# Nine small pieces of the blocks' weights, one an iteration, behind the evacuation of heads

## The reference, cut to what matters

```
x = x + gate_a * (attend(ln_mod(x) @ W_qkv + b_qkv) @ W_proj + b_proj)
x = x + attend(ln(x) @ W_qc + b_qc, context @ W_kvc + b_kvc) @ W_cproj + b_cproj
x = x + gate_m * (gelu(ln_mod(x) @ W_mlp1 + b_mlp1) @ W_mlp2 + b_mlp2)
```

## Time and profile before

| | |
|---|---|
| median of three runs | 2992.5 us (2986.59 to 2997.8) |
| the profiled execution | 2997.99 us |
| its span | 2996.2 us |
| TensorE busy | 2816.4 us (94%) |
| VectorE, ScalarE, GpSimd busy | 59%, 51%, 23% |
| mean granted TensorE clock | 0.96 |

### The profile page before, as it was taken

The page is one execution under the profiler, slowest core; times in us unless marked ns, Lnnn a source line. Parts: engine busy times, 40 slices in busy tenths (PEclk is TensorE's granted clock), DMA queues, the critical chain, the costliest instruction groups (busy, mean ns, idle before and its releaser), DMA issues. The chain is left out here.

```text
span 2996.2 us, 61868 instructions
## 1 busy us (share of the span) xinstructions
PE 2816.4 (94%) x23508; PEld 2298.0 (77%) x23508; DVE 1761.6 (59%) x3583; ACT 1535.1 (51%) x2701; POOL 700.9 (23%) x760
## 2 busy tenths in 40 slices
PE   5999999994899999999999999999999999999997
PEld 4999999993577777777777776777777777777766
DVE  1344444433567756766766756676675676666642
ACT  2444444432365546556556555556555655655653
POOL 3334443321121212212212211122121221221211
PEclk8999999996799989999999998999999999999998
DMA  5122111003343344444453443434445444444421
GB/s 166 64 76 88 67 67 39 24 8 112 71 109 103 94 108 98 103 102 119 111 130 93 109 101 99 101 88 112 120 98 135 99 94 110 96 94 109 98 63 34
DMA packets 276262, 277.90 MB, mean 93 GB/s; under 512 B 90176, under 2 KB 205232, under 8 KB 275968
## 3 DMA queue, kind: packets, MB, share of 16 engines
q1 hardware_dynamic: 260176, 251.24, 33.7%
q10 hardware_dynamic: 15792, 22.70, 2.5%
HBM read 99.03 MB, written 29.56 MB: 43 GB/s over the span
## 5 line engine op out<-in xcount | busy, mean ns | idle before, releaser
L1538 ACT ACTIVATE p_f<-score 128x1024 f32<-128x1024 f32 (+1 forms) x576 | 560.7, 1019 | 369.4 <-PE obank L2159 175.7
L1815 DVE TENSOR_REDUCE m_a<-score 128x4 f32<-128x1024 f32 x384 | 457.6, 1217 | 58.8 <-PE score L2125 58.7
L2229 PE MATMUL gbank<-w,h_c 128*128 128x256 f32 x1536 | 414.2, 405 | 1.2 <-ACT h_c L1555 0.9
L2229 PEld LDWEIGHTS gbank<-w,h_c 128*128 128x128 f32 x1536 | 283.7, 197 | 51.1 <-issue 1.3
L959 PE MATMUL m_ps<-m_comb,m_w 128*128 128x256 f32 x2304 | 300.5, 286 | 0.0
L959 PEld LDWEIGHTS m_ps<-m_comb,m_w 128*128 128x128 f32 x2304 | 284.8, 190 | 3.1 <-issue 1.7
L1419 POOL TENSOR_TENSOR res_a<-res_a,bias_a 128x512 f32<-128x512 f32 x48 | 64.7, 1347 | 710.0 <-DMA bias_a<-rows_L 710.0
L632 ACT ACTIVATE m_hf<-m_ps,tab 128x256 f32<-128x256 f32 x192 | 80.5, 470 | 252.7 <-PE m_ps L959 252.7
L2159 PE MATMUL obank<-p_f,v_s 128*20 128x256 f32 x3072 | 206.9, 401 | 0.0
L574 POOL TENSOR_TENSOR m_hhl<-m_hf,m_hhl 128x512 fp32r<-128x512 f32 x96 | 125.3, 1305 | 327.8 <-DVE m_hhl L798 327.8
L1825 DVE TENSOR_REDUCE m_b<-gbank 128x4 f32<-128x308 f32 x192 | 92.2, 480 | 170.8 <-PE gbank L2174 108.9
(11 more groups left out here) (234 smaller groups left out, 5627.9 us busy)
## 6 DMA issues: line engine op xcount, KB each, us to landing
k_cat<-k_hl SPq DMA_DIRECT2D x288, 128.0 KB, 3.6
q_cat<-q_hl SPq DMA_DIRECT2D x288, 128.0 KB, 4.0
qc_cat<-qc_hl SPq DMA_DIRECT2D x288, 128.0 KB, 3.2
split_L<-m_cut SPq DMA_DIRECT2D x24, 512.0 KB, 5.3
x_a<-x_after_L SPq DMA_DIRECT2D x48, 256.0 KB, 4.0
res_a<-x_after_L SPq DMA_DIRECT2D x48, 256.0 KB, 2.8
kc_cat<-kc_hl SPq DMA_DIRECT2D x288, 39.0 KB, 1.9
x_after_L<-y_c SPq DMA_DIRECT2D x32, 256.0 KB, 3.2
```

Of the source, the lines that this page charges most:

```text
L1538: e.activation(p_f[i % 4][0:n, :], score[i % 2].ap[0:n, :, :].rearrange("p h n -> p (h n)"), ACT.Exp, scale=SCALE).then_inc(ex.sem, 1)
L1815: e.tensor_reduce(m_a[:, :, i::NPAIR].rearrange("p t h -> p h t"), score[i % 2].ap[:, :, :].rearrange("p h (t k) -> p h t k", t=TT), AX.X, ...
L2229: mm = e.matmul(B_DOWN.ap[:, tt, :], h_c[:, k, tt * P:(tt + 1) * P], weights_of(d)["w2"][:, k, :], start=(k == 0), stop=(k == MC - 1))
```

## The change

The two-place weights come in nine loads a layer: the three spread biases, `w_kvc` in two halves (256 KB each) and `w2` in four pieces (256 KB each). `next_rest` issues one of them an iteration, in n = 6 to 14 for layer 2 and n = 23 to 31 for layer 3, and its place in ScalarE's list is behind `self_heads(a, 0)`. `next_up_high` stands behind it. `next_self_out` moves behind `self_heads(a, 1)`, `next_queries_keys` behind `cross_max_high`, and `next_up_low` to the end of the previous iteration, behind `cross_keys_high`. The bias columns of all three layers get buffers of their own and are loaded by SyncE in layer 0, in its iterations 8 to 17. SyncE's loads for layer 1 come in the same nine pieces, in iterations 2 to 6.

```diff
-            loads.append((w["bv"][:, :], spread(bv)))
-            loads.append((w["bvc"][:, :], spread(bvc)))
-            loads.append((w["boc"][:, :], spread(p["boc"])))
-            side_by_side(w["kvc"], p["kvc"])
-            loads.append((w["w2"][:, :, :], chunks(p["w2"])))
+            loads = [(w[k][:, :], spread(b)) for k, b in (("bv", bv), ("bvc", bvc), ("boc", p["boc"]))]
+            for i in range(2):
+                loads.append((w["kvc"][:, :, i * D:(i + 1) * D], chunks(kvc[i])))
+            for i in range(0, MC, 2):
+                loads.append((w["w2"][:, i:i + 2, :], chunks(p["w2"][i * P:(i + 2) * P, :])))
             return loads
+
+        def column_loads(L):
+
+            p = layer_parts(L)
+            if L < 3:
+                b = [p["bqkv"][0:D], p["bqkv"][D:2 * D], p["bqc"], p["bkvc"][0:D]]
+            else:
+                b = [p["bq"], p["bk"], p["bqc"], p["bkc"]]
+            return ([(bcols[L][:, 2 * i:2 * i + 2], column(b[i])) for i in range(4)]
+                    + [(bcols[L][:, 8:16], column(p["b1"]))])
...
-        n_w = [0, 10, 10, 11]
+        n_w = [0, 9, 9, 9]
...
+                if n >= 8:
+                    for dst, src in columns[n - 8::N_ITER - 8]:
+                        e.dma_start(dst, src).then_inc(S["col"].sem, 16)
...
-                                      bias=weights_of(u)["bcol"][:, at + m:at + m + 1])
+                                      bias=bcols[layer(u)][:, at + m:at + m + 1])
...
-                if 6 <= n < 11:
-                    for dst, src in layer_loads(2)[n - 6::5]:
+                if 6 <= n < 15:
+                    for dst, src in layer_loads(2)[n - 6::9]:
                         e.dma_start(dst, src).then_inc(s_w[2], 16)
...
-                if NB + 7 <= n < NB + 13:
-                    for dst, src in layer_loads(3)[n - NB - 7::6]:
+                if NB + 7 <= n < NB + 16:
+                    for dst, src in layer_loads(3)[n - NB - 7::9]:
                         e.dma_start(dst, src).then_inc(s_w[3], 16)
...
                 exp_table(n - 6)
-                next_self_out(n - 4)
-                next_rest(n)
-                next_up_low(n - 6)
                 self_weights(a, 0)
                 self_weights(a, 1)
                 queries_high(n - 2)
                 self_weights(a, 2)
                 self_weights(a, 3)
-                next_up_high(n - 6)
                 self_weights(a, 4)
                 self_weights(a, 5)
                 self_weights(a, 6)
                 self_weights(a, 7)
+                cross_max_high(b)
                 next_queries_keys(n - 2)
-                cross_max_high(b)
+                self_heads(a, 0)
                 next_cross_queries(n - 4)
-                self_heads(a, 0)
+                next_rest(n)
+                next_up_high(n - 6)
                 self_heads(a, 1)
+                next_self_out(n - 4)
                 next_cross_out(n - 5)
...
                 cross_keys_high(a)
+                next_up_low(c)
                 self_modulated(q)
```

More of the change, by code:

```diff
@@ L107, in build @@
         cond_siluT = sbr("cond_siluT", [P, CC, NB])
+        bcols = [None] + [sbr(f"b_col{i}", [P, 16]) for i in (1, 2, 3)]
         tabs = [None] + [sbr(f"tab{i}", [P, NB, 8]) for i in (1, 2, 3)]
@@ L112, in layer_buffers @@
             return dict(
-                kvc=sb(f"w_kvc{i}", [P, CC, 2 * D]), w2=sb(f"w_2{i}", [P, MC, D]), bcol=sb(f"b_col{i}", [P, 16]),
+                kvc=sb(f"w_kvc{i}", [P, CC, 2 * D]), w2=sb(f"w_2{i}", [P, MC, D]),
                 bv=sb(f"b_v{i}", [P, D]), bvc=sb(f"b_vc{i}", [P, D]), boc=sb(f"b_oc{i}", [P, D]))
@@ L142, in layer_loads @@
         def layer_loads(L):
[L144 to L150, removed]
+            w, p = WT[L % 2], layer_parts(L)
             if L < 3:
-                bq, bk, bv = (p["bqkv"][i * D:(i + 1) * D] for i in range(3))
-                bkc, bvc = (p["bkvc"][i * D:(i + 1) * D] for i in range(2))
-            else:
[L156 to L159, removed]
-            loads.append((w["bv"][:, :], spread(bv)))
-            loads.append((w["bvc"][:, :], spread(bvc)))
-            loads.append((w["boc"][:, :], spread(p["boc"])))
-            side_by_side(w["kvc"], p["kvc"])
-            loads.append((w["w2"][:, :, :], chunks(p["w2"])))
-            return loads
+                bv, bvc = p["bqkv"][2 * D:3 * D], p["bkvc"][D:2 * D]
+                kvc = [p["kvc"][0][:, at:at + D] for at in (0, D)]
+            else:
+                bv, bvc, kvc = p["bv"], p["bvc"], p["kvc"]
+            loads = [(w[k][:, :], spread(b)) for k, b in (("bv", bv), ("bvc", bvc), ("boc", p["boc"]))]
[3 more added lines that the diff above has]
+                loads.append((w["w2"][:, i:i + 2, :], chunks(p["w2"][i * P:(i + 2) * P, :])))
+            return loads
+        def column_loads(L):
[6 more added lines that the diff above has]
+                    + [(bcols[L][:, 8:16], column(p["b1"]))])
         def own_load(L, k):
@@ L183, in build @@
             mixture(nc, t, mix, layer_loads(1), s_w[1],
-                    [own_load(1, k) for k in ("o", "oc")], pieces(1) + pieces(2) + pieces(3), split, xs[0], rows, consts, chunks, spread, by_tile, buffers)
+                    [own_load(1, k) for k in ("o", "oc")], pieces(1) + pieces(2) + pieces(3), split,
+                    column_loads(1) + column_loads(2) + column_loads(3), xs[0], rows, consts, chunks, spread, by_tile, buffers)
         WT[0] = layer_buffers(root, 0)
-        blocks(nc, t, xs, tabs, rows, ident, half, eps5, eps6, WT, s_w, n_w, layer_loads,
+        blocks(nc, t, xs, tabs, bcols, rows, ident, half, eps5, eps6, WT, s_w, n_w, layer_loads,
                W, W_in, split, own_load, by_tile, buffers)
@@ L406, in _, with mixture @@
             e.tensor_scalar(mix["b2"][:, 2, :], ps_b[1][:, 0, :], 0.5, None, ALU.mult).then_inc(s_done, 1)
-def mixture(nc, t, mix, loads_L1, s_w1, own_L1, raw_pieces, split, x_out, rows, consts, chunks, spread, by_tile, buffers):
+def mixture(nc, t, mix, loads_L1, s_w1, own_L1, raw_pieces, split, columns, x_out, rows, consts, chunks, spread, by_tile, buffers):
     from concourse import mybir
@@ L460, in mixture @@
                         ve=1, rstd=1, nxlo=1, evlo=1, hl=6, y=1, cuthi=1, cutlo=1),
-                    dma=dict(x0=1, x1=1, x2=1, ctx=1, store=1, wtab0=1, wtab1=1, brow=2, orow=1, ar=1, raw0=1, raw1=1, cut0=1, cut1=1))
+                    dma=dict(x0=1, x1=1, x2=1, ctx=1, store=1, wtab0=1, wtab1=1, brow=2, orow=1, ar=1, raw0=1, raw1=1, cut0=1, cut1=1, col=1))
         raw_in, cut_out = [S[f"raw{i}"] for i in range(2)], [S[f"cut{i}"] for i in range(2)]
@@ L552, in _ @@
             e.wait_ge(*S["orow"].at(len(gates) - 1))
+            e.wait_ge(*S["col"].at(len(columns) - 1))
             for i in range(2):
@@ L1109, in _, with blocks @@
                 table_group(f)
-def blocks(nc, t, xs, tabs, rows, ident, half, eps5, eps6, WT, s_w, n_w, layer_loads, W, W_in, split, own_load, by_tile,
+def blocks(nc, t, xs, tabs, bcols, rows, ident, half, eps5, eps6, WT, s_w, n_w, layer_loads, W, W_in, split, own_load, by_tile,
            buffers):
@@ L1555, in up_act @@
                     ac = e.activation(h_c[:, m, :], B_UP[i].ap[:, j, :], gelu,
-                                      bias=weights_of(u)["bcol"][:, 8 + m:9 + m])
+                                      bias=bcols[layer(u)][:, 8 + m:9 + m])
                 ac.then_inc(S["C_h"].sem, 1)
@@ L1786, in low_part @@
                     n = view(m).shape[1]
-                    lo = e.scalar_tensor_tensor(dst[:, 1, m, 0:n], view(m), weights_of(u)["bcol"][:, at + m:at + m + 1],
+                    lo = e.scalar_tensor_tensor(dst[:, 1, m, 0:n], view(m), bcols[layer(u)][:, at + m:at + m + 1],
                                                 dst[:, 0, m, 0:n].bitcast(F32), ALU.add, ALU.subtract)
```

## The result

The changed kernel takes 2952.18 us (median of four runs, 2949.02 to 2954.21), against 2989.8 us for the kernel before (four runs, 2986.59 to 2997.8). The ratio is 0.9873, with a 95% interval of 0.9853 to 0.9894: 37.6 us or 1.3% faster. The first three runs of the kernel before are those of the table ahead of the prediction (median 2992.5 us); the fourth took 2987.09. The profiled execution of the changed kernel took 2951.26 us. The prediction was 2953.

The account below looks back on a forecast made before the run. TensorE was taken to set the pace at 44.81 us an iteration, with seven iterations lengthened by late query copies. -42.7 + 2.0 + 0.9 = -39.8 us from the 2992.5 median gave 2953 us, range 2944 to 2968.

Parts of the forecast that it names:

- The sum: Total over the whole kernel: -42.7 for the long iterations, +2.0 for the new place, +0.9 for x_a: -39.8 us.
- part (4): Columns from the blocks and early layer 0 become 15 SyncE issues in layer 0; layer 1 weights in pieces: 0 us.
- The seven prices: Excess of seven long block iterations with weight loads over 44.81 us each: 1.59 to 10.49, together 42.7 us.
- the second stretch: Undisturbed run of 11 block iterations, read as 493.86 us, used for the 44.81 us mean iteration.
- Part (1): next_rest moved some 21 us into the iteration, one piece each: removes 31.6 us, new place costs 2.0 us.
- Part (2): w_up loads moved at layer changes: 11.1 us go; x_a delayed 0.45 us twice, late q_cat priced at 0.
- rival D: Piece at 21 us makes the second qc_cat<-mT_b copy late, halving the clock: 132 us, 3082 us; chance 0.03.
- signs of being wrong: A new wait over 1 us at L2139 or L2188, or a half-clock stretch between 850 and 2880 us.
- these five prices: Excess of the five long iterations loading w_kvc or w2 at next_rest's old place: 31.6 us together, expected to vanish.
- B: next_up_low at the iteration's end makes q_cat<-mT_a or qc_cat late at both layer changes: about 2965 us; chance 0.09.
- C: Bytes beside the copies cost, not the place: 18 pieces at 1.59 us, 28.6 us, giving 2979; chance 0.06.
- E: The long iterations have their own cause and late copies only follow; time stays at 2992 us; chance 0.02.

Follow-up runs that it names:

- The pieces at the old place: Changed kernel with next_rest alone back behind exp_table, still in nine pieces, columns still in layer 0: 2952.38 us, ratio 0.9872 to the kernel before.
- the place alone: Kernel before with only next_rest moved behind self_heads(a, 0); large loads, columns on ScalarE's queue, w_up at its old place: 2967.94 us, ratio 0.9925.
- the columns alone: Changed kernel with next_rest back behind exp_table and large loads again (512 KB, 1 MB); columns still in layer 0: 2975.31 us, ratio 0.9943.
- the pieces alone: Changed kernel with next_rest back behind exp_table in nine pieces, layers 2 and 3 columns on ScalarE's queue ahead of pieces: 2964.66 us, ratio 0.9919.
- the place and pieces: Changed kernel with only the columns of layers 2 and 3 back on ScalarE's queue, five ahead of a piece per layer: 2954.18 us, ratio 0.9867.

## Why the prediction was right, and where its reasons were not

**The sum.** It said -39.8 us; the medians differ by 37.6. Taken in the profiles, the 43 iterations from 906 to 2873 us before took 1967.05 us, those of the changed kernel 1925.04: 42.0 us less, where the forecast has -42.7 + 2.0 + 0.9 = -39.8.

```profile
906.11:2873.16 1967.05, 1905.26 (x16594) 1471.71 (x16592) 1323.38 (x2603) 1127.34 (x1890) 397.53 (x465) 0.98 0.44 105
```

```profile
904.03:2829.07 1925.04, 1876.18 (x16594) 1455.88 (x16592) 1322.71 (x2603) 1127.69 (x1890) 396.67 (x465) 1.00 0.46 107
```

The spans differ by 46.7. Of the 4.7 us outside these 43 iterations, 2.1 lie before them and 2.6 behind. Behind them no load of the change stands, and 1.5 us of the 2.6 come and go between two profiles of the changed kernel: its last whole iteration, in which the pipeline drains, took 43.76 us in one and 45.28 in the other (45.24 in the kernel before). Before them lie layer 0, with the columns and pieces of part (4), and the first piece of `next_rest`; whether these have a share in the 2.1 us stays open.

That the profiles show more than the medians has a reason that the sum did not allow for: the profiled run before took 2997.99 us, 8.2 above the median of four. The seven prices are those of a long run, and the forecast took all of them off the median. Against the median of three that it started from, the kernel gained 40.3 us; against that of four, 37.6. That the sum lies between the two is in part luck.

One reading of the earlier trace rows is off, by little: the eleventh iteration of the second stretch ends at 2829.93 us, not at 2831.80. An undisturbed iteration is then (447.21 + 491.99) / 21 = 44.72 us, and the seven prices are 43.3 us, not 42.7.

**The prices.** All seven went: the seven iterations are 42.5 us shorter, of the 42.7 forecast. **Part (1)'s new place** was sized 2.0 and measured 0. **Part (2)** was right in both halves: `x_a` waited 0.45 us longer, twice, and in the two iterations into which `next_up_low` reaches neither `q_cat<-mT_a` nor `qc_cat<-qc_hl` was late. Putting `w_up` back cost 11.5 us, against 11.1 less 0.9. The small waits for `qc_cat<-mT_b` were inside rival D's mechanism, at 0.3 to 1.0 us each, far below its 2.3.

**The signs.** All that were named for the waits, the seven iterations, the pieces and `x_a` came. Of the signs of being wrong one was nearly met: the new wait at L2188 is 0.97 us, just under 1. The other was met by the letter: a stretch at the lower clock does lie before 2880 us, in the iteration from 2829.07 to 2872.83 us (0.92). But that is the drain of the pipeline, which the kernel before has too, later (0.89, from 2873 us), and not a price of the change.

**What failed** is the sentence that 256 KB was enough for 1.59 and for 7.31 us at the old place, so that "the place does the harm". The pieces at the old place refute it: 2952.38 us, the same as with the move. The step is sound for 1 MB (55.32 us without a column), and wrong for 256 KB: there the harm came with the bias column ahead of the piece on the same queue. Part (4) priced those columns in the blocks at 0, by their issue on ScalarE alone, and did not ask what they do to the transfer behind them. The forecast of these five prices was not luck alone: the new place by itself wins all of them but 6.3 us (the place alone). But it would have come out the same without the move, and that it came out whole is owed to the pieces and the columns, which the working priced at nothing.

**What holds in its place.** There are three ways to be harmless at `next_rest`, and the change takes all three. With the pieces, either no column ahead of them (2952.38) or the new place (2954.18) is enough. With the large loads, the new place and no columns leave 2 to 4 us, too little to tell by the times (2957.16); at the old place they cost 20 to 22 us (2975.31). Each of the three alone leaves a part of the loss: the columns alone 20 to 22 us, the pieces alone 12, the place alone some 4, an estimate from 2967.94 less the 11.5 of `w_up`, which was at its old place there. So the move of `next_rest`, the centre of the forecast, gains nothing on top of the other two; the move of `w_up` gains its 11.5 us.

**Rivals.** B did not happen. C is refuted in its sum: 18 pieces beside the copies at the old place cost nothing either, not 28.6 us. That bytes beside the copies cost is so for 1 MB. D and E did not happen. The page of the Trainium skill "DMA: Bandwidth & Descriptors", Bandwidth, which advises at least 1 MiB a batch, would have kept `w2` whole; at the old place and without columns, 1 MB took 9.6 us to land and cost 10.5 us, and its four pieces took 3.0 to 3.4 us each and cost none. Its rule is about the rate of the transfer, and here only the copies beside it counted.

**Left open:** whether a column harms the piece behind it by its 256 to 1024 small packets in the ring, or by starting the piece 0.44 us later and so nearer to the `qc_cat` copies. A later start without a column was not tried. What speaks against it as the whole cause is the place and pieces: there no `qc_cat` copies are near, and the pieces behind a column landed 1.4 us later all the same (in the median of the ten). And the column of 1024 packets did no more harm than those of 256, which speaks against the number of packets. The kernel before with only `w_up` moved was not tried either.

## What to carry to other kernels

Price a load by the small, critical transfers that fly beside it, not by its own time: find where they are issued and how much slack their first user has, and keep each load so small that it delays them by less than that, or put it where none is due soon. Here the slack for `qc_cat` is some 1.3 us, an estimate from the iteration at 1098.08 us of the kernel before: the last of the six copies is issued at 1106.0 and lands 3.4 us later, and the first matmul that needs them starts at 1110.77. Look also at what stands ahead of a load on its own queue. When a change does several things at once, a right total says nothing about which of them did it.

## What the runs showed of the hardware

- A bias column of 1 to 4 KB, issued ahead of a 256 KB load on the same queue, made it land later. At the old place ten such loads took 3.6 to 6.9 us behind the column, ten took 2.7 to 3.9 with the column behind them, and twelve took 3.0 to 3.8 with none. At the new place it was 3.4 to 5.3 us behind a column and 2.6 to 3.2 with none.
- A short wait can cost several times itself, or not. Of two iterations of the kernel before with half of `w_kvc` each, one waited 1.2 us for `qc_cat`, stayed at the full 2.4 GHz and took 46.40 us; the other waited 1.1 us, fell to 1.2 GHz for a stretch and took 52.12. Behind a wait of 3.2 us, and behind the one of 3.02 in the columns alone, the clock was halved too, so that 1 MB cost 10.5 us by a wait of 3. The length of the wait alone does not decide it: in the place alone, an iteration with a wait of 2.54 us stayed at the full clock and took 47.09 us.
